# Two edge aggregations: GpSimd's wait for seven of the preceding eight gathers, at every second step only

## The chip, the cores and the metric

The kernel runs on one core of one Trainium2 chip. The metric is the device time of one execution in microseconds (us). Before the change the median of 3 runs is 7060.26 us (7059.98 to 7061.63).

## The reference

The reference is two layers of a graph network on N = 6250 nodes with 256 features each. A layer adds to x a graph attention over E = 200000 edges and a dense mixing of the same rows, and then a mixture of experts. Only the two graph attentions bear on the change. Cut to what matters, layer 0 has

```python
hW = h @ W + b                                   # 6250 x 64
e = leaky_relu(s[row, head] + d[col, head])      # per edge and head, 4 heads
alpha = softmax of e over the edges of one row
out[row, head] += alpha * hW[col]                # sum over the row's edges
```

Layer 1 is the same in form, with a table row of 256 values per node (4 heads x 64) in place of 64. Each edge needs the table row of its column node, and the edges come in no order of columns: this is a gather of 200000 rows, once in each layer.

## The kernel before, in words

The edges are sorted by destination on the chip and padded to 1616 tiles of 128 edges. `stage_aggregate` runs once for each layer (tags `_0` and `_1`, table rows of 68 and of 260 floats). It works in 202 **steps** of KT = 8 tiles, that is 1024 edges, and four steps (STEP_RING = 4, slots r = 0 to 3) make a **turn**. Turn 0 and the last turn (two steps) are written out, the 49 turns between them are a hardware loop.

In every step

- GpSimd (POOL) issues eight indirect DMAs, one for each tile, L876. Each fetches 128 table rows by the indices `st_idx` into `got[:, r, k, :]`, the slot r of a ring of four. The first seven count up the semaphore `gathered[r]`, the eighth `last_in[r]`.
- SyncE loads `spread`, the row numbers of the step's edges, broadcast to all partitions (L893).
- VectorE (DVE) makes the one-hot matrices `hot` (L975) and `hot_t` (L982), and waits for the eight gathers before it reduces the row scores (L993) and makes the exponents `z` (L1002 to L1004, in layer 1 from L995 on).
- ScalarE exponentiates (L909, L912), and DVE scales the gathered rows into `weighted` (L1016), which counts up `scaled`. 
- TensorE (PE) sums the weighted rows by destination with `hot` (L952), DVE adds the sums to `acc` (L1024), and PE makes the scores of a later step (L937).
- Besides, each step takes a part of the layer's dense mixing with it (the "guest": `BallMix` in layer 0, `GateMix` in layer 1), on PE, ACT and DVE. From the middle of the second aggregation the guest is in another phase ("out").

What sets the order on GpSimd is in `gather`, L866 to L877. Before the eight gathers of step j it waits for three things: that ScalarE has staged the step's indices (`idx_staged`), that DVE has scaled step j - 4, so that the slot is free (`scaled`), and that the first seven gathers of step j - 1 have landed (`gathered` of the slot before, L874):

```python
pool.wait_ge(idx_staged, j + 1)
if not first:
    pool.wait_ge(scaled, j - (STEP_RING - 1))
if not first or r > 0:
    t, q = (turn, r - 1) if r else (turn - 1, STEP_RING - 1)
    pool.wait_ge(gathered[q], t * (16 * (KT - 1)) + 16 * (KT - 1))
```

DVE has its own waits for `gathered[r]` and `last_in[r]` ahead of L993.

Of the kernel before, what the change touches and what calls it, by code (L numbers as in the profile page):

```python
# [770 lines left out]
def stage_aggregate(nc, g, tag, table, width, shared, rows, row_list, acc, top, guest):  # L771
# [10 lines left out]
    with stage(nc) as own:  # L782
# [49 lines left out]
        def steps_of(last):  # L832
            return range(ENDING if last else STEP_RING)
# [30 lines left out]
        @block.gpsimd  # L864
        def _(pool):
            def gather(turn, r, first):  # L866
                j = turn * STEP_RING + r
                pool.wait_ge(idx_staged, j + 1)
                if not first:
                    pool.wait_ge(scaled, j - (STEP_RING - 1))  # L870
                if not first or r > 0:
                    t, q = (turn, r - 1) if r else (turn - 1, STEP_RING - 1)
                    pool.wait_ge(gathered[q], t * (16 * (KT - 1)) + 16 * (KT - 1))
                pool.nop(nofuse=True)  # L874
                for k in range(KT):
                    pool.indirect_dma_start(got[:, r, k, :], None, table,  # L876
                                            bass.IndirectOffsetOnAxis(ap=st_idx[:, r, k:k + 1], axis=0))\  # L877
                        .then_inc(gathered[r] if k < KT - 1 else last_in[r], 16)
            for r in range(STEP_RING):
                gather(0, r, True)  # L880
            with pool.Fori(1, TURNS - 1) as turn:
                for r in range(STEP_RING):
                    gather(turn, r, False)
            for r in steps_of(True):
                gather(TURNS - 1, r, False)
# [2287 lines left out]
```

## Time and profile before

| | |
|---|---|
| median of the runs | 7060.26 us |
| profiled execution | 7063.9 us, of which span 7062.1 us |
| first aggregation, first to last gather | 495.4 to 2733 us |
| second aggregation, first to last gather | 3581.8 to 5861.5 us |
| busy share of the span | PE 72%, DVE 62%, POOL 49%, ACT 25% |
| mean granted TensorE clock | 0.83 |

A profile is one execution. Busy is the time in which an engine executes. Idle before an instruction is put down to what ended it: a DMA's landing, another engine's instruction, or "issue", where the profile shows no event that ended it. [...] A wait itself is executed by the engine's sequencer and is idle time of the engine.

### The profile page before, as it was taken

Reading aid. Unit: us, or ns where it says so; the run is one execution under the profiler, and the core shown is the slowest. Engines: PE = TensorE matmul, PEld = TensorE weight load, DVE = VectorE, ACT = ScalarE, POOL = GpSimd, SP = SyncE. Lnnn points to the kernel's source line nnn. Section 1 sums busy time; section 2 is a strip of 40 time slices with the busy share of each in tenths; the row PEclk is TensorE's granted clock in tenths of the full one; section 3 lists DMA queues with packets and bytes.
Section 4 is the critical chain, followed back from the end, with each engine's and each line's share of the span. In section 5 each row is a group of like instructions: output and inputs, shape, how many; then the busy total and the mean of one; then the engine's idle time right before and its main releaser. Section 6 shows DMA issues by size and latency. Waiting matters only on the chain. (4 is left out here: it accounts for less than half of the span.)

```text
span 7062.1 us, 90296 instructions
## 1 busy us (share of the span) xinstructions
PE 5095.9 (72%) x21196; PEld 3660.6 (52%) x21197; DVE 4389.3 (62%) x8953; ACT 1783.8 (25%) x4856; POOL 3469.1 (49%) x3669
## 2 busy tenths in 40 slices
PE   1446666666666664699766666667777777999999
PEld 1445555555555552466534444445555555666666
DVE  8987777777777778722566655556666667333333
ACT  7322222222222222222310000001111113433332
POOL 0126767666767766144146666666666664000000
PEclk8668888888888886799878887877777777999999
DMA  1022222222222222322444444444444444000001
GB/s 55 22 44 51 52 52 52 52 51 52 52 52 52 52 51 58 116 64 64 145 135 124 125 123 123 123 124 130 130 132 132 132 131 114 5 5 4 9 4 36
DMA packets 380644, 534.45 MB, mean 76 GB/s; under 512 B 119264, under 2 KB 240119, under 8 KB 380407
## 3 DMA queue, kind: packets, MB, share of 16 engines
q0 software_dynamic: 139648, 299.92, 17.8%
q1 hardware_dynamic: 240886, 233.29, 11.2%
q8 instruction: 43, 0.70, 0.0%
q14 instruction: 67, 0.54, 0.0%
HBM read 475.96 MB, written 56.96 MB: 75 GB/s over the span
## 5 line engine op out<-in xcount | busy, mean ns | idle before, releaser
L876 POOL DMA_INDIRECT got<-table,st_idx x3232 | 3092.9, 957 | 1453.5 <-issue 1004.8
L952 PE MATMUL ps_sum<-weighted,hot 128*128 128x260 f32 x6464 | 1861.2, 447 | 143.2 <-DVE acc L1024 139.0
L952 PEld LDWEIGHTS ps_sum<-weighted,hot 128*128 128x128 f32 x6464 | 1403.1, 229 | 563.0 <-DVE acc L1024 228.8
L1024 DVE TENSOR_TENSOR acc<-acc,ps_sum 128x260 f32 x1664 | 707.1, 425 | 890.3 <-PE ps_sum L952 750.0
L937 PE MATMUL ps_score<-score_split,hot_t 128*128 x3232 | 250.1, 188 | 1294.7 <-DVE z L1004 1267.5
L937 PEld LDWEIGHTS ps_score<-score_split,hot_t 128*128 128x128 bf16 x3232 | 196.8, 103 | 1471.7 <-issue 1456.7
L1016 DVE TENSOR_TENSOR weighted<-got,ps_weight 128x2048 f32<-128x2048 f32 x404 | 921.5, 2281 | 4.3 <-ACT weighted L912 0.8
L909 ACT ACTIVATE ps_weight<-z 128x32 f32<-128x32 f32 x404 | 81.2, 201 | 2969.8 <-DVE z L1004 2969.8
L3058 DVE SCALAR_TENSOR_TENSOR x_res<-ps_yf,comb,x_res 128x256 f32 x392 | 189.7, 484 | 638.0 <-PE ps_yf L2966 638.0
L975 DVE TENSOR_TENSOR hot<-ps_score,row_loc 128x1024 f32<-128x1024 f32 x404 | 492.1, 1218 | 3.5
L993 DVE TENSOR_REDUCE row_score<-ps_score 128x64 f32<-128x192 f32 (+1 forms) x404 | 163.3, 404 | 520.3 <-DMA got<-table,st_idx 518.9
L2946 PE MATMUL ps_hf<-acc,ws_f 128*128 (+2 forms) x896 | 348.2, 542 | 6.0 <-ACTq L2993 6.0
L2966 PE MATMUL ps_yf<-ws_f,h2t 128*128 128x256 f32 x1568 | 347.7, 379 | 0.8 <-ACT h2t L3006 0.8
L2946 PE MATMUL ps_hf<-h1t,ws_f 128*128 128x384 f32 (+1 forms) x896 | 346.0, 539 | 0.8 <-ACT h1t L3006 0.8
L2966 PEld LDWEIGHTS ps_yf<-ws_f,h2t 128*128 128x128 f32 x1568 | 297.8, 190 | 53.6 <-ACT h2t L3006 1.4
L3006 ACT ACTIVATE h2t<-ps_hf,own_scale 128x512 f32<-128x512 f32 x224 | 162.3, 725 | 507.9 <-PE ps_hf L2946 507.9
L2946 PEld LDWEIGHTS ps_hf<-acc,ws_f 128*128 128x128 f32 x896 | 171.1, 191 | 173.6 <-issue 114.8
L2946 PEld LDWEIGHTS ps_hf<-h1t,ws_f 128*128 128x128 f32 x896 | 170.2, 190 | 156.0 <-issue 107.1
L263 POOL TENSOR_TENSOR shifted<-xs,pivot 128x256 f32<-128x256 f32 x49 | 43.1, 880 | 382.4 <-DVE pivot L401 230.5
L1283 PE MATMUL ps_mix<-mix_xin,wq 128*128 128x128 f32 x1176 | 227.5, 379 | 0.4
L1283 PEld LDWEIGHTS ps_mix<-mix_xin,wq 128*128 128x128 f32 x1176 | 217.7, 289 | 3.7
L1939 POOL DMA_INDIRECT y_rows<-y_e,slot_home x108 | 106.6, 987 | 209.6 <-DVE y_e L2030 205.0
(533 smaller groups left out, 7558.3 us busy)
## 6 DMA issues: line engine op xcount, KB each, us to landing
spread<-row_list SPq DMA_DIRECT2D x404, 256.0 KB
got<-table,st_idx POOLq DMA_INDIRECT x3232, 2.8
gate_xin<-ball_rows SPq DMA_DIRECT2D x98, 128.0 KB
got_y_e<-y_rows SPq DMA_DIRECT2D x10, 896.0 KB
table<-row_e SPq DMA_DIRECT2D x50, 130.0 KB, 2.6
ball_rows<-xt SPq DMA_DIRECT2D x10, 640.0 KB, 4.7
mix_xin<-ball_rows SPq DMA_DIRECT2D x49, 128.0 KB
xn_rows<-xs_m SPq DMA_DIRECT2D x49, 128.0 KB, 1.7
```

Of the source, the lines that this page charges most:

```text
L876: pool.indirect_dma_start(got[:, r, k, :], None, table, bass.IndirectOffsetOnAxis(ap=st_idx[:, r, k:k + 1], axis=0))\
L937: last = nc.tensor.matmul(scores[:, k, :], hot_t[:, r % 2, k, :], split[:, :, :, :].rearrange("p t a c -> p (t a c)")[:, ds(b * SP, SP)], ...
L952: last = nc.tensor.matmul(ps_g[:, p % 2, 0:AW], hot[:, r % 2, k, :], weighted[:, r % 2, k, :], start=(k == n * p), stop=(k == n * p + n - 1))
L975: nc.vector.tensor_tensor(hot[:, r % 2, :, :], count_to.unsqueeze(1).to_broadcast([P, KT, P]), g.row_loc[:, ds(i * KT, KT)].unsqueeze(2).t ...
L993: link(nc.vector.tensor_reduce(row_score[:, :, :], scores.rearrange("p k (a c) -> p k c a", a=PARTS), AX.X, ALU.add))
L1016: nc.vector.tensor_tensor(out, v, w, ALU.mult).then_inc(scaled, 1)
L1024: nc.vector.tensor_tensor(acc[:, ds(b * AW, AW)], acc[:, ds(b * AW, AW)], ps_g[:, p % 2, 0:AW], ALU.add).then_inc(added, 1)
L1283: last = nc.tensor.matmul(bank[:, m * P:(m + 1) * P], self.mix.wq[:, c, (m0 + m) * P:(m0 + m + 1) * P], self.xin[:, c, :], start=(c == 0), ...
L2946: last = nc.tensor.matmul(ps_h[:, j, 0:HALVES[hf][1]], ws[:, par, l, c, f * P:(f + 1) * P], rhs(c, hf), start=(c == 0), stop=(c == 1))
L2966: last = nc.tensor.matmul(ps_y[:, k % 4, 0:D], h2[:, c, k * P:(k + 1) * P], ws[:, par, 2, c, :], start=(c == 0), stop=(c == 1))
L3006: nc.scalar.activation(h[:, f, at:at + n], ps_h[:, j, 0:n], ACT.Relu, bias=own_s[:, par, 1, l, f:f + 1], scale=own_s[:, par, 0, l, f:f + 1])\
L3058: nc.vector.scalar_tensor_tensor(xr, ps_y[:, k % 4, 0:D], comb[:, ds(t * 8 + pair * 2 + par, 1)], xr, ALU.mult, ALU.add).then_inc(y_used, 1)
```

## The change

The wait on `gathered` stands at r = 0 and r = 2 only. At r = 1 and r = 3 the other two waits remain.

```diff
-                if not first or r > 0:
+                if r % 2 == 0 and not (first and r == 0):
                     t, q = (turn, r - 1) if r else (turn - 1, STEP_RING - 1)
                     pool.wait_ge(gathered[q], t * (16 * (KT - 1)) + 16 * (KT - 1))
```

GpSimd's instructions in the loop over the turns, before, from behind the gathers of r = 0 on. A semaphore stands under the first name that its number had in the program: iotas_made is `idx_staged`, x_loaded is `scaled`, and eps0_set, b_wide_ready, w0_prepared and wl_ready are `gathered` of slots 3, 0, 1 and 2, for which the steps r = 0, 1, 2 and 3 wait.

```order
L868 REGISTER_ALU
L870 REGISTER_ALU [waits iotas_made]
L873 ISA [waits x_loaded]
L876 DMA got<-table,st_idx 128x68 [waits b_wide_ready]
L876 DMA got<-table,st_idx 128x68 x7
L868 REGISTER_ALU
L870 REGISTER_ALU [waits iotas_made]
L876 DMA got<-table,st_idx 128x68 [waits x_loaded,w0_prepared]
L876 DMA got<-table,st_idx 128x68 x7
L868 REGISTER_ALU
L876 DMA got<-table,st_idx 128x68 [waits wl_ready,iotas_made,x_loaded]
L876 DMA got<-table,st_idx 128x68 x7
```

And the same piece with the change:

```order
L868 REGISTER_ALU
L870 REGISTER_ALU [waits iotas_made]
L876 DMA got<-table,st_idx 128x68 [waits x_loaded]
L876 DMA got<-table,st_idx 128x68 x7
L868 REGISTER_ALU
L870 REGISTER_ALU [waits iotas_made]
L873 ISA [waits x_loaded]
L876 DMA got<-table,st_idx 128x68 [waits w0_prepared]
L876 DMA got<-table,st_idx 128x68 x7
L868 REGISTER_ALU
L876 DMA got<-table,st_idx 128x68 [waits iotas_made,x_loaded]
L876 DMA got<-table,st_idx 128x68 x7
```

The first gather of r = 1 no longer waits for slot 0's gathers, and that of r = 3 no longer for slot 2's. No gather moves; the empty instruction L873 only goes to another step. The same holds for the second aggregation, whose rows read 128x260.

The first turn, which is written out ahead of the loop, as the difference of the two:

```order
 L876 DMA got_0<-table0,st_idx_0 128x68 [waits iotas_made]
 L876 DMA got_0<-table0,st_idx_0 128x68 x7
-L876 DMA got_0<-table0,st_idx_0 128x68 [waits iotas_made,b_wide_ready]
+L876 DMA got_0<-table0,st_idx_0 128x68 [waits iotas_made]
 L876 DMA got_0<-table0,st_idx_0 128x68 x7
 L876 DMA got_0<-table0,st_idx_0 128x68 [waits iotas_made,w0_prepared]
 L876 DMA got_0<-table0,st_idx_0 128x68 x7
-L876 DMA got_0<-table0,st_idx_0 128x68 [waits iotas_made,wl_ready]
+L876 DMA got_0<-table0,st_idx_0 128x68 [waits iotas_made]
 L876 DMA got_0<-table0,st_idx_0 128x68 x7
```

Here too only the waits of the second and the fourth step are gone. Of the 201 such waits of an aggregation 101 go and 100 stay. The other engines' instructions are the same.

## Rows read from the trace of the kernel before

**Rows 1.** Costliest groups: busy us, mean ns of one | idle before it, its enders.

```profile
L876 POOL DMA_INDIRECT got<-table,st_idx x3232 | 3092.9, 957 | 1453.5 <-issue 1004.8 <-DMA got<-table,st_idx 398.6 <-ACT st_idx L904 32.1
```

**Rows 2.** Busy by stretch: us, PE PEld DVE ACT POOL (count), PEclk, DMA share, GB/s.

```profile
497.00:2734.00 2237.00, 1496.74 (x7455) 1221.13 (x7456) 1641.97 (x2810) 594.20 (x2021) 1558.14 (x1615) 0.83 0.25 52
3583.00:4710.00 1127.00, 751.72 (x2866) 486.48 (x2866) 680.67 (x1296) 77.74 (x395) 758.15 (x799) 0.80 0.45 124
4710.00:5862.00 1152.00, 856.51 (x3169) 621.62 (x3169) 723.61 (x1434) 216.74 (x548) 773.98 (x817) 0.75 0.47 130
```

**Rows 3.** POOL's timeline, start us, us, [idle before]: one turn, second aggregation, r = 0 first.

```profile
4304.57 0.94 POOL L876 DMA_INDIRECT got<-table,st_idx  x1 [1.34 <-DMA got<-table,st_idx]
...
4313.32 0.94 POOL L876 DMA_INDIRECT got<-table,st_idx  x1 [0.30 <-issue]
4315.75 0.95 POOL L876 DMA_INDIRECT got<-table,st_idx  x1 [1.48 <-DMA got<-table,st_idx]
...
4324.50 0.95 POOL L876 DMA_INDIRECT got<-table,st_idx  x1 [0.30 <-issue]
4326.76 0.94 POOL L876 DMA_INDIRECT got<-table,st_idx  x1 [1.31 <-issue]
...
4335.51 0.94 POOL L876 DMA_INDIRECT got<-table,st_idx  x1 [0.30 <-issue]
4337.84 0.94 POOL L876 DMA_INDIRECT got<-table,st_idx  x1 [1.39 <-DMA got<-table,st_idx]
```

**Rows 4.** Groups of L876 without the first gather: first aggregation, then the second.

```profile
L876 POOL DMA_INDIRECT got<-table,st_idx x1615 | 1558.1, 965 | 678.4 <-issue 494.8 <-DMA got<-table,st_idx 165.5 <-DVE weighted L1016 17.4
L876 POOL DMA_INDIRECT got<-table,st_idx x1615 | 1532.1, 949 | 746.4 <-issue 510.0 <-DMA got<-table,st_idx 233.1 <-ACT st_idx L904 2.7
```

**Rows 5.** POOL's timeline: four of the 36 long gaps at a step's second gather.

```profile
653.26 0.95 POOL L876 DMA_INDIRECT got<-table,st_idx  x1 [1.68 <-issue]
...
1503.87 0.94 POOL L876 DMA_INDIRECT got<-table,st_idx  x1 [1.68 <-issue]
...
1626.01 0.94 POOL L876 DMA_INDIRECT got<-table,st_idx  x1 [1.68 <-issue]
...
5853.10 0.94 POOL L876 DMA_INDIRECT got<-table,st_idx  x1 [1.67 <-issue]
```

**Rows 6.** Groups of L993: first aggregation, then the second to 4710, then from 4710.

```profile
L993 DVE TENSOR_REDUCE row_score<-ps_score 128x64 f32<-128x192 f32 x201 | 71.4, 355 | 297.4 <-DMA got<-table,st_idx 296.9
L993 DVE TENSOR_REDUCE row_score<-ps_score 128x96 f32<-128x288 f32 x99 | 45.0, 455 | 147.1 <-DMA got<-table,st_idx 147.0
L993 DVE TENSOR_REDUCE row_score<-ps_score 128x96 f32<-128x288 f32 x102 | 46.1, 452 | 75.8 <-DMA got<-table,st_idx 75.0
```

**Rows 7.** Timeline of DVE and PE around one wait for gathers, second aggregation.

```profile
5218.12 0.48 DVE L982 TENSOR_SCALAR hot_t<-spread,lane 128x1024 bf16<-128x1024 bf16 x1
...
5221.32 0.46 DVE L993 TENSOR_REDUCE row_score<-ps_score 128x96 f32<-128x288 f32 x1 [2.72 <-DMA got<-table,st_idx]
...
5223.03 0.62 PE L937 MATMUL ps_score<-score_split,hot_t 128*128 x8 [4.75 <-DVE z L1004]
```

**Rows 8.** Who waited for whom: us in total, times, longest us; whole span.

```profile
POOL got L876 <- ACT st_idx L904: 32.1, 13, 16.4
...
POOL got L876 <- DVE weighted L1016: 18.0, 16, 1.6
```

**Rows 9.** L876 over the span: duration ns min/median/max; then time to landing.

```profile
L876 POOL DMA_INDIRECT got<-table,st_idx x3232: 938/944/1446, 495.4 to 5860.6; - x191
...
DMA to landing us min/median/max: 2.3/2.8/4.7
```

**Rows 10.** Timeline, first aggregation: a gather beside hot_t; the group of hot_t.

```profile
1522.86 0.48 DVE L982 TENSOR_SCALAR hot_t<-spread,lane 128x1024 bf16<-128x1024 bf16 x1
1522.98 1.17 POOL L876 DMA_INDIRECT got<-table,st_idx  x1 [0.30 <-issue]
...
L982 DVE TENSOR_SCALAR hot_t<-spread,lane 128x1024 bf16<-128x1024 bf16 x202 | 101.6, 503 | 0.1
```

## The prediction

> **What bounds the kernel now.** I read the busy shares by stretch first, then the groups of gathers, then GpSimd's timeline of single steps, and last what the consumers wait for. In the two aggregations no engine is full: by stretch PE is busy 67 to 74% of the time, DVE 60 to 73%, GpSimd 67 to 70%, and the DMA engines 25 to 47% [rows 2]. A busy share does not tell the bound here, since GpSimd's gathers come one after another with fixed gaps. The 3232 gathers are busy for 3092.9 us and have 1453.5 us of idle time before them, which together is the length of both aggregations [rows 1]. So the step is as long as eight gathers and the gaps before them.
>
> The timeline shows what the gaps are [rows 3]. Within a step each gather follows the last one after 0.30 us, which no event ended: about 0.94 + 0.305 = 1.25 us per gather, 10.0 us per eight. Ahead of the first gather of a step the gap is 1.31 to 1.48 us, and what ends it is the landing of gathers. That is the wait on `gathered`: the seventh gather of the step before lands some time after the eighth has been issued, and the sequencer then starts the next one. The turn repeats in all 50 turns of an aggregation. (The row at 4326.76 says "issue", but its wait is the same one; so "issue" holds a part of these pauses.)
>
> That the gathers set the end is seen on the other side: DVE waits for them ahead of L993 for 296.9 us in the first aggregation and for 147.0 + 75.0 us in the second [rows 6]. During such a wait PE does nothing either: its next matmul, the score, comes after 4.75 us of idle time and is released by the same DVE's `z` [rows 7]. A shorter wait is thus a shorter step, not one that PE fills.
>
> **The change part by part.** Removed are 101 pauses in each aggregation, at r = 1 and r = 3. Nothing is added: no gather, no DMA and no instruction of another engine, and on GpSimd's queue nothing is moved past anything. With the wait gone, the first gather of such a step should follow like the others, after 0.305 us, since the two waits that remain were nearly always over long before: `scaled` ended a gap 16 times in 404 steps, 18.0 us in all, and `idx_staged` 13 times, 32.1 us, of which 16.4 us is a single wait at the stage's start [rows 8].
>
> First aggregation: idle time before 1615 gathers is 678.4 us [rows 4]. Less 1615 x 0.305 = 492.6 us of plain gaps, 185.8 us are left. A second kind of gap has to come off: 18 times the second gather of a step comes after 1.68 us in place of 0.30 [rows 5], 18 x 1.37 = 24.7 us. So 161.1 us belong to 201 pauses, 0.80 us each over the plain gap. Half of them go: **81 us**.
>
> Second aggregation: 746.4 - 492.6 - 24.7 = 229.1 us, 1.14 us each; half is **115 us**. In the turn shown the odd pauses are the longer ones, 1.48 + 1.39 against 1.34 + 1.31 us [rows 3], less 0.305 each 2.26 against 2.04 us, 5% over the mean of both: **+5 us**.
>
> The kept pauses, at r = 0 and r = 2, I cost at no change: they end by the landing of the seventh gather of the step before, median 2.8 us after issue [rows 9], and gathers already follow each other at 1.25 us in each run of eight. So two or three are under way at any time, then as now, though 16 come in a run. The DMA engines are busy 45 to 47% in the second aggregation [rows 2]; some 5% more in the same time does not fill them.
>
> What is late next is DVE, with PE behind it. Its wait for gathers is the cover that the gain can use up: 296.9 us for 81 in the first aggregation, 147.0 for about 59 in the first half of the second, but 75.0 for about 61 in the second half, where the guest is heavier [rows 6]. DVE is not late in every step there, and the ring of four slots evens out only neighbours; carrying the 102 steps forward with DVE's own time per step as it is and the gathers earlier, I find that 8 us are not given back: **-8 us**.
>
> Sum: 81 + 115 + 5 - 8 = 193 us. Against the profiled execution's 7063.9 us this is 6871 us; the median stands 3.6 us below that execution, so I predict **6867 us** (-2.7%). Bounds of the sum: at best nothing is lost to DVE and the clock, granted at 0.75 in the last stretch [rows 2], comes up with the shorter idle times to the 0.80 of the stretch before. That shortens PE's 856.5 us there by 54 us; I let a third of it count, since DVE waits for PE only in part, and the gain is 193 + 8 + 19 = 220 us, about 6840 us. At worst that stretch gives back nothing, 193 - 53 = 140 us (61 less the 8 already off), 6920 us.
>
> One thing in the trace speaks against the change. A gather is longer where DVE's `hot_t` starts just before it: 1.17 us beside the 0.94 us of the others, and up to 1.446 us, a lengthening of 0.50 us, as long as a `hot_t` takes [rows 9, 10]. Now some `hot_t` fall into a pause of GpSimd, where they cost nothing. The means of 965 and 949 ns against the median of 944 [rows 4, 9] put today's cost at 34 and 8 us. With a random place of `hot_t` in the step I expect about the same, and enter 0; the worst is that each of the 202 steps without a pause meets a full one, 202 x 0.50 = 101 us, which the rivals take up. [...]
>
> **The rivals.**
>
> *DVE and PE take it back* (8%). In the second half of the second aggregation PE is busy 74%, and DVE's waits on gathers are down to 75.0 us in 102 steps [rows 2, 6]. If its time per step grows where the wait shrinks, that half gains nothing: 6920 us. Against it stands that PE idles during the waits [rows 7].
>
> *The lock costs what the pause saved* (3%): 193 - 101 = 92 us gained, 6968 us. For it: the rows on `hot_t`. Against it: most gathers beside a `hot_t` show no lengthening (the mean in the second aggregation is 949 ns).
>
> *The wait only changes its name* (3%): `scaled` or `idx_staged` would be reached at once, and the time is 7060 us within 14. Against it are the few times that either ended a gap [rows 8].
>
> *Slower: long runs of gathers cost a stall* (6%). Once in 88 gathers, 18 times in each aggregation, the gap at L876 is 1.68 us though nothing is waited for [rows 5]; from 1503.87 to 1626.01 are 88 gathers. Something is counted there. If it is descriptors that pile up while GpSimd does not pause, and the pauses now clear it, a run of 16 would meet such a stall each time: 202 x 1.37 = 277 us against 193 gained, 7144 us. It decides for slower from a stall in 70% of the runs (193 / 277). Against it: 88 gathers hold eleven of today's pauses, the interval is the same in both aggregations though their transfers differ almost fourfold in size, and within a run of eight the eighth gather takes no longer than the first, 0.94 us [rows 3].
>
> **How the numbers follow.** The forecast has 80%, the rivals 8, 3, 3 and 6%. The range is 6840 to 6945 us: the bounds of the sum, 6840 and 6920, with 25 us above for a part of the lock's price. It holds the first rival and nearly all of the forecast's chance; left out are the other rivals and some 5% of the forecast. A measurement of this kernel can tell about 0.2%, 14 us, from no change. Faster by more than that: 80 + 8 + 3 = 91%; within it 3%; slower 6%.
>
> **What would show it.** Right: in the first gathers of r = 1 and r = 3 the gap is 0.30 us, in those of r = 0 and 2 it stays at 1.0 to 1.4; L876 idles some 80 us less in the first aggregation and 115 to 120 less in the second; the aggregations take about 2157 and 2168 us; DVE's wait at L993 falls to about 215 and 110 us, and all other stages stay as they are. Wrong: gathers longer than 965 ns in the mean (lock); more than 36 gaps of 1.68 us (stall); gaps at r = 1 and 3 that end by `weighted` or `st_idx` (another name); GpSimd idle less but the second aggregation no shorter (DVE and PE). Kept pauses that grow by as much as the others shrink would refute the costing of landings.

## The result, and the profile after

The changed kernel takes 6814.94 us (median of 4 runs, 6807.93 to 6820.05), the kernel before 7060.53 us in the same comparison: a ratio of 0.9651, 95% interval 0.9635 to 0.9668. It is 246 us faster, where 193 us were forecast, and the time lies 25 us below the range. The profiled execution is the lowest of the four, 6807.93 us with a span of 6806.1 us, so the two traces differ by 256 us.

Busy time by stretch of the changed kernel, as in [rows 2]: us, busy of PE, PEld, DVE, ACT and POOL with counts, granted TensorE clock, share of the DMA engines, GB/s. The first row is the first aggregation, the other two are the halves of the second.

```profile
494.50:2613.00 2118.50, 1463.42 (x7445) 1189.48 (x7445) 1637.79 (x2812) 593.29 (x2021) 1544.21 (x1616) 0.85 0.25 55
3466.00:4533.00 1067.00, 727.22 (x2898) 483.46 (x2898) 688.22 (x1308) 78.10 (x398) 766.35 (x808) 0.82 0.48 133
4533.00:5602.00 1069.00, 829.13 (x3125) 599.61 (x3125) 711.76 (x1412) 215.49 (x543) 765.45 (x808) 0.77 0.50 138
```

From first to last gather the aggregations now take 2118.7 and 2136.9 us, before 2238.0 and 2279.8: 119 and 143 us less, and all the rest of the kernel 6 us more. The granted clock is up by 0.02 in each stretch: 0.85, 0.82 and 0.77, before 0.83, 0.80 and 0.75 [rows 2].

GpSimd's timeline over one turn of the second aggregation, r = 0 first, as in [rows 3]:

```profile
4142.25 0.94 POOL L876 DMA_INDIRECT got<-table,st_idx  x1 [1.25 <-DMA got<-table,st_idx]
...
4151.00 0.95 POOL L876 DMA_INDIRECT got<-table,st_idx  x1 [0.30 <-issue]
4152.26 0.95 POOL L876 DMA_INDIRECT got<-table,st_idx  x1 [0.30 <-issue]
...
4163.31 0.95 POOL L876 DMA_INDIRECT got<-table,st_idx  x1 [1.25 <-DMA got<-table,st_idx]
...
4173.30 0.95 POOL L876 DMA_INDIRECT got<-table,st_idx  x1 [0.30 <-issue]
...
4184.34 0.94 POOL L876 DMA_INDIRECT got<-table,st_idx  x1 [1.34 <-DMA got<-table,st_idx]
```

The steps r = 1 (4152.26) and r = 3 (4173.30) begin 0.30 us after the last gather, like any other gather; r = 0 and r = 2 still pause. The gathers' groups of the two aggregations, to be held against [rows 4]:

```profile
L876 POOL DMA_INDIRECT got<-table,st_idx x1615 | 1543.4, 956 | 573.8 <-issue 472.5 <-DMA got<-table,st_idx 98.9 <-DVE weighted L1016 1.8
L876 POOL DMA_INDIRECT got<-table,st_idx x1615 | 1531.8, 948 | 603.9 <-issue 470.6 <-DMA got<-table,st_idx 127.5 <-DVE weighted L1016 4.9
```

And DVE's wait for gathers, in the groups over the whole span, against [rows 6]:

```profile
L993 DVE TENSOR_REDUCE row_score<-ps_score 128x64 f32<-128x192 f32 (+1 forms) x404 | 162.7, 403 | 340.7 <-DMA got<-table,st_idx 339.8
```

The idle time fell by 104.6 and 142.5 us, more than the 81 and 120 us that the removed pauses were to bring. And in the first aggregation the gathers themselves are shorter, 956 ns for 965, 14.7 us in all. DVE still waits for gathers, 339.8 us for 519.

Where the rest of the idle time went is seen at the long gaps of [rows 5]. The first gathers of the steps 14, 25 and 36, with the second gather of each:

```profile
640.46 0.94 POOL L876 DMA_INDIRECT got<-table,st_idx  x1 [1.00 <-DMA got<-table,st_idx]
643.08 1.19 POOL L876 DMA_INDIRECT got<-table,st_idx  x1 [1.68 <-issue]
...
756.40 0.94 POOL L876 DMA_INDIRECT got<-table,st_idx  x1 [0.30 <-issue]
757.65 0.94 POOL L876 DMA_INDIRECT got<-table,st_idx  x1 [0.30 <-issue]
...
871.11 0.94 POOL L876 DMA_INDIRECT got<-table,st_idx  x1 [0.96 <-DMA got<-table,st_idx]
873.72 0.94 POOL L876 DMA_INDIRECT got<-table,st_idx  x1 [1.68 <-issue]
```

Before, each of these steps had a gap of 1.68 us ahead of its second gather. Now step 25, which begins without a wait, has none. Nine are left in each aggregation, all in steps that begin with a wait, where 18 were before.

The third source is the pause that was kept. The mean gap ahead of a step's first gather, taken over all steps of the trace, in us:

| | first aggregation, r = 0 and 2 | r = 1 and 3 | second, r = 0 and 2 | r = 1 and 3 |
|---|---|---|---|---|
| before | 1.118 | 1.101 | 1.384 | 1.514 |
| changed | 0.998 | 0.305 | 1.301 | 0.305 |

The kept pauses are 0.12 and 0.08 us shorter, 100 of each. So three things had to be explained: long gaps, kept pauses and shorter gathers.

### The profile page after: what moved, and what is told of

Read it like the earlier page. It is cut to its first block and busy times, and to the rows that moved or that the text cites. A ratio compares the mean times of both kernels' runs of the same rounds, so it can differ in the third digit from the quotient of the medians.

```text
span 6806.1 us, 90196 instructions
## 1 busy us (share of the span) xinstructions
PE 5017.1 (74%) x21196; PEld 3608.0 (53%) x21197; DVE 4385.5 (64%) x8953; ACT 1781.6 (26%) x4856; POOL 3454.1 (51%) x3669
## 5 line engine op out<-in xcount | busy, mean ns | idle before, releaser
L876 POOL DMA_INDIRECT got<-table,st_idx x3232 | 3077.8, 952 | 1205.1 <-issue 943.1
L1016 DVE TENSOR_TENSOR weighted<-got,ps_weight 128x2048 f32<-128x2048 f32 x404 | 921.5, 2281 | 4.3 <-ACT weighted L912 0.8
L993 DVE TENSOR_REDUCE row_score<-ps_score 128x64 f32<-128x192 f32 (+1 forms) x404 | 162.7, 403 | 340.7 <-DMA got<-table,st_idx 339.8
## 6 DMA issues: line engine op xcount, KB each, us to landing
spread<-row_list SPq DMA_DIRECT2D x404, 256.0 KB
```

Of the source, the lines that this page charges most:

```text
L876: pool.indirect_dma_start(got[:, r, k, :], None, table, bass.IndirectOffsetOnAxis(ap=st_idx[:, r, k:k + 1], axis=0))\
L993: link(nc.vector.tensor_reduce(row_score[:, :, :], scores.rearrange("p k (a c) -> p k c a", a=PARTS), AX.X, ALU.add))
L1016: nc.vector.tensor_tensor(out, v, w, ALU.mult).then_inc(scaled, 1)
```

## The experiments

**The wait at the odd steps** in place of the even ones.

```diff
-                if not first or r > 0:
+                if r % 2 == 1:
```

> The wait stands at r = 1 and r = 3 only, the other half of the steps; nothing is left out. After the change 9 long gaps of 1.68 us at a step's second gather were left in each aggregation, at the steps 14, 36, 58 and so on, where 18 stood before, at 14, 25, 36 and so on. Theory A (every eleventh step the sequencer is held up for about 1.4 us whatever the step; it shows only where the sequencer has just come out of a wait and has nothing issued ahead): 9 long gaps in each aggregation, but now at the odd steps 25, 47, 69. Theory B (the hold-up belongs to the number of pauses, one for each eleven of them): 9 gaps at even steps again, or at steps of another interval. The kept pauses now are those at r = 1 and 3, which met the spread loads before: theory C (a kept pause is longer where a spread load is under way) expects them at 1.1 us in the first and 1.4 to 1.5 us in the second aggregation, against 1.00 and 1.30 in the changed kernel, and a time of 6820 to 6850 us; if the spread loads don't matter, 1.00 and 1.30 us and the time of the changed kernel, 6815 us.

6849.3 us, ratio 0.9706 (0.9689 to 0.9722). Steps 14 and 25 again, in this kernel's timeline of GpSimd:

```profile
640.73 0.94 POOL L876 DMA_INDIRECT got<-table,st_idx  x1 [0.31 <-issue]
641.98 0.96 POOL L876 DMA_INDIRECT got<-table,st_idx  x1 [0.30 <-issue]
...
756.27 0.95 POOL L876 DMA_INDIRECT got<-table,st_idx  x1 [1.04 <-DMA got<-table,st_idx]
758.89 0.94 POOL L876 DMA_INDIRECT got<-table,st_idx  x1 [1.67 <-issue]
```

Theory A holds: the gap went from step 14 to step 25, and on to 47, 69 and so on, nine in each aggregation. The hold-up is there every eleventh step, and it shows only behind a wait. Why is seen in the sequencer's own rows. When its branch at the end of a turn is executed, gathers that it has issued have not yet begun on the engine: four or five in the kernel before and here, eight to ten in the changed kernel. So a delay of 1.37 us (1.68 - 0.305) is covered by gathers already issued. Directly behind a wait nothing is: in the trace before, each of the 402 waits ends after the last gather issued ahead of it (at one of them 4303.86 against 4303.22 us, and the next gather begins at 4304.57). The covered hold-up shows there too: in the first aggregation of the changed kernel it is eight gathers in the turns 11, 22, 33 and 44, whose last steps 47, 91, 135 and 179 are such eleventh steps without a wait, and ten in all the other 45 turns of the loop.

The kept pauses are 1.058 us in the first aggregation (1.1 was expected) and 1.533 in the second (1.4 to 1.5). In the first, those of r = 3 now end by `scaled` for the most part, 46.7 us. Of the first aggregation's pauses those of r = 1, which end by a landing, stand at 1.002, so 1.1 us was not met there. With nearly the same number of waits (101 in place of 100) this kernel is 34 us slower than the change: which half of the waits is kept matters. The largest part is idle time ahead of the second aggregation's gathers, 628.8 us against 603.9; gathers that are 12 and 4 us longer in sum, 1555.2 and 1536.0 us, add to it.

**No wait at all** on the preceding gathers.

```diff
-                if not first or r > 0:
-                    t, q = (turn, r - 1) if r else (turn - 1, STEP_RING - 1)
-                    pool.wait_ge(gathered[q], t * (16 * (KT - 1)) + 16 * (KT - 1))
```

> The wait on the preceding step's gathers stands nowhere; only the waits for the indices and for the free slot are left. Nothing is left out. Theory (each pause costs its gap less 0.305 us, and the long gaps are hidden wherever there is no pause): no gap over 0.31 us at a step's first gather save for late indices or slots, no gap of 1.68 us, gathers at 1.25 us each. From the changed kernel's 6815 us the first aggregation gains 70 us of pauses and 12 of long gaps; the second has 100 us of pauses and 12 of long gaps, but DVE waits only 110.6 us for gathers in its first half and 30.0 in its second, so I expect 55 and 25 there: 6650 us, range 6620 to 6700, with GpSimd now waiting for DVE's scaled in the last stretch. Rival (with no pause at all gathers pile up at the DMA engines): landings of 4 us or more in the median against 2.7, gathers longer than 952 ns in the mean, and a time of 6815 us or more.

6634.01 us, ratio 0.9401 (0.9386 to 0.9417), inside the range: 424 us faster than the kernel before, at 7057.51 us in that comparison, and some 180 us faster than the change, so the best version here. The groups of its gathers, first and second aggregation (the line is 873 here):

```profile
L873 POOL DMA_INDIRECT got<-table,st_idx x1615 | 1543.4, 956 | 492.5 <-issue 492.5
L873 POOL DMA_INDIRECT got<-table,st_idx x1615 | 1536.7, 952 | 492.4 <-issue 491.5 <-DVE weighted L1013 0.9
```

The view of that line's instructions over the span, with their duration (min/median/max in ns) and the time to landing:

```profile
L873 POOL DMA_INDIRECT got<-table,st_idx x3232: 943/947/1445, 494.5 to 5411.0; - x191
...
DMA to landing us min/median/max: 2.3/2.8/5.2
```

All idle time left in each aggregation is 1615 gaps of 0.305 us. No long gap is left, the sequencer is twelve gathers ahead at the end of every turn, gathers land after 2.8 us in the median as before, and their means of 956 and 952 ns are those of the changed kernel within 4 ns. The rival of piled-up gathers falls. My expectation that DVE would hold GpSimd back in the last stretch fell too: `scaled` ended a wait for 0.9 us in all. DVE is later at the very end instead: its last add to `acc` ends 38.4 us after the last gather of the second aggregation, where it was 24.5 us in the kernel before.

**Small spread loads**, all waits kept.

```diff
-                sp.dma_start(spread[:, r % SPREAD_RING, :], row_list[ds(i, 1), :].to_broadcast([P, KT * P])).then_inc(spread_in[r % SPREAD_RING], 16)
+                n, q = P if first and r < SPREAD_RING else 16, r % SPREAD_RING
+                sp.dma_start(spread[0:n, q, :], row_list[q:q + 1, :].to_broadcast([n, KT * P])).then_inc(spread_in[q], 16)
```

> The kernel before, all waits kept, but from the third step on the load of spread fills 16 partitions in place of 128, always with the row numbers of step 0 or 1: row scores of all later steps are those of wrong rows, so this part of the computation is left out. SyncE issues the same number of loads at the same places. Theory C (a pause is longer where a spread load delays the seventh gather's landing): the long pauses go, the mean pause falls from 1.109 us to about 1.00 in the first and from 1.449 to about 1.30 us in the second aggregation, both at even and at odd steps; 22 + 30 = about 50 us less in all, near 7010 us. If the spread loads don't matter the pauses stay at 1.11 and 1.45 us and the time at 7060 us.

7044.46 us in a single run, 13 us under the median of the kernel before in that comparison (7057.51). The gathers' groups:

```profile
L876 POOL DMA_INDIRECT got<-table,st_idx x1615 | 1567.5, 971 | 659.8 <-issue 490.2 <-DMA got<-table,st_idx 168.0 <-DVE weighted L1017 1.0
L876 POOL DMA_INDIRECT got<-table,st_idx x1615 | 1532.8, 949 | 735.9 <-issue 506.2 <-DMA got<-table,st_idx 227.6 <-ACT st_idx L905 2.1
```

The mean pauses are 0.993 (even steps) and 1.038 us (odd) in the first aggregation, 1.307 and 1.484 in the second. At the even steps that is what the changed kernel shows, 0.998 and 1.301, so the spread loads did make these pauses longer. But 50 us were expected, and two things take them away: the gathers of the first aggregation came out longer, 971 for 965 ns, which gives 9 of its 19 us back, and the odd pauses of the second hardly moved: 1.484 us is also what other kernels with all waits there show (1.479 in run e4, 1.481 in run e6). Another cause had to be there.

**Small loads of the guest too.** In the kernel before, SyncE's load of `gate_xin` is issued beside the seventh gather of an even step, at 4312.07, and the pause behind it is 1.48 us [rows 3]:

```profile
4311.88 0.33 SPq L2467 DMA_DIRECT2D gate_xin<-ball_rows  x1
4312.07 0.95 POOL L876 DMA_INDIRECT got<-table,st_idx  x1 [0.30 <-issue]
```

```diff
-            sp.dma_start(self.xin[:, h, :, :], mix.f_t[ds(j, 1), :, :, :].rearrange("o p c n -> (o p) c n")).then_inc(self.x_in, 16)
+            n = 16
+            sp.dma_start(self.xin[0:n, h, :, :], mix.f_t[ds(j, 1), 0:n, :, :].rearrange("o p c n -> (o p) c n")).then_inc(self.x_in, 16)
```

(and the same for tile i, from the third on)

> As the run with the small spread loads (all waits kept, row numbers left out from the third step on), and besides the guest's loads of gate_xin in the second aggregation fill 16 partitions in place of 128 from the third tile on, so that the dense mixing of layer 1 is left out in part too. With small spread loads alone the pauses of the second aggregation stayed at 1.46 and 1.51 us at r = 1 and 3, against 1.31 and 1.30 at r = 0 and 2, and gate_xin is issued at every second step, about when the seventh gather is. Theory C, widened to all of SyncE's loads: 1.30 us at r = 1 and 3 too, about 18 us less in the second aggregation, 7025 us. If gate_xin is not the cause: 1.46 and 1.51 us as there, and 7044 us.

7030.01 us in a single run. The same turn in its timeline, r = 1, 2, 3 and 0:

```profile
4295.96 0.95 POOL L876 DMA_INDIRECT got<-table,st_idx  x1 [1.30 <-DMA got<-table,st_idx]
...
4306.97 0.94 POOL L876 DMA_INDIRECT got<-table,st_idx  x1 [1.32 <-issue]
...
4318.10 0.94 POOL L876 DMA_INDIRECT got<-table,st_idx  x1 [1.45 <-DMA got<-table,st_idx]
...
4329.15 0.95 POOL L876 DMA_INDIRECT got<-table,st_idx  x1 [1.29 <-DMA got<-table,st_idx]
```

r = 1 is down from 1.46 to 1.33 us in the mean and on the level of r = 0 and 2 (1.31); r = 3 fell from 1.51 to 1.43 and keeps 0.12 us over them. So a load of SyncE beside the seventh gather goes with a later landing, and the pause shows it. For `spread`: in the trace before the seventh gather lands 2.735 us after its start where a load is issued within the 1.75 us behind that start, and 2.507 us after it elsewhere (even pauses of the first aggregation; 3.038 and 2.790 in the second), with the small loads of run e3 2.496 and 2.437 (2.824 and 2.762). For `gate_xin`, at the odd pauses of the second aggregation: 3.103 and 2.875 us in run e1, whose loads are whole, 2.820 and 2.782 here. The rest at r = 3 is open; it is there in the first aggregation too (1.10 against 1.00 at r = 1), whose guest loads were left as they are.

**More instructions on GpSimd**, to see what the long gap counts.

```diff
+                for _ in range(4):
+                    pool.sem_inc(spare, 1)
                 pool.wait_ge(idx_staged, j + 1)
```

> The kernel before, all waits kept, with four increments of a spare semaphore more on GpSimd ahead of each step's waits. Nothing is left out. It asks what the long gap of 1.68 us counts, which comes every eleventh step, 88 gathers apart. If gathers (or their descriptors) are counted: 18 long gaps in each aggregation, still 88 gathers apart. If instructions of GpSimd's sequencer are counted: more of them, closer together, 88 x 46 / 62 = about 65 gathers apart and some 24 in each aggregation, at places that are no longer always the second gather. The time is 7060 us plus at most 12 us either way; each increment itself takes some tens of ns of the sequencer, which runs ahead of the engine.

7059.03 us in a single run. The trace has the increments: each takes 17 ns on GpSimd's sequencer, the four begin 78 ns apart, and at most steps the first is executed when five gathers of the step before have not yet begun on the engine (GpSimd's rows at L870 and L879). The long gaps stay 18 in each aggregation, 88 gathers apart, at the second gather of the same steps; step 25 here (the line is 879):

```profile
773.13 0.95 POOL L879 DMA_INDIRECT got<-table,st_idx  x1 [1.67 <-issue]
```

Not the number of instructions sets the interval but that of gathers, or something each of them brings. The first long gap stands ahead of the 114th gather in both aggregations, so a count of gathers does not run on from one aggregation to the next (1832 indirect DMAs lie between, no multiple of 88). What is done in these 1.4 us stays open.

**Another form of hot_t**, all waits kept.

```diff
-                nc.vector.tensor_scalar(..., spread[:, r % SPREAD_RING, :], g.lane[:, 0:1], None, ALU.is_equal)
+                nc.vector.tensor_tensor(..., spread[:, r % SPREAD_RING, :], g.lane[:, 0:1].to_broadcast([P, KT * P]), ALU.is_equal)
```

> The kernel before, all waits kept, with hot_t made by a tensor_tensor of spread and a broadcast of lane in place of the tensor_scalar with a scalar operand; nothing is left out. DVE needs about 1.2 us for it in place of 0.503 (the tensor_tensor that makes hot takes 1.218). Theory D (the tensor_scalar on bf16, and not any DVE work, lengthens a gather that begins beside it): the mean gather falls from 965 to 950 ns in the first aggregation (a rest stays beside L1016 and L1423) and from 949 to 946 in the second, and the time by the 24 + 5 us that this makes of 2 x 1616 gathers, less what a longer DVE step gives back: 7030 to 7055 us. Rival (any DVE operation at that place lengthens it, or it is the place in the step): the means stay at 965 and 949 and the time at 7060 or some us above, for 0.7 us more of DVE per step.

7145.13 us, ratio 1.0126 (1.0109 to 1.0143), slower, and neither theory had that. The groups of gathers and of hot_t over the span:

```profile
L876 POOL DMA_INDIRECT got<-table,st_idx x3232 | 3216.5, 995 | 1408.9 <-issue 1009.1 <-DMA got<-table,st_idx 348.0 <-ACT st_idx L904 32.8
L982 DVE TENSOR_TENSOR hot_t<-spread,lane 128x1024 bf16<-128x1024 bf16 x404 | 491.4, 1217 | 5.9 <-DMA spread<-row_list 5.6
```

One pair of them in its timeline:

```profile
3705.76 1.22 DVE L982 TENSOR_TENSOR hot_t<-spread,lane 128x1024 bf16<-128x1024 bf16 x1
3705.83 1.95 POOL L876 DMA_INDIRECT got<-table,st_idx  x1 [1.31 <-DMA got<-table,st_idx]
```

The gather that begins 0.07 us after hot_t lasts 1.95 us in place of 0.94, so it is about 1 us longer, beside a hot_t that still had 1.15 us to run. Theory D, that only the tensor_scalar does this, falls: the tensor_tensor does it too, and for longer. The busy time of all gathers is up by 123.6 us (3216.5 - 3092.9), shorter gaps give 44.6 us back (1453.5 - 1408.9), which together is 79 us; the traced span is up by 79.9 us (7062.1 to 7142.0), the median by 89 us. So here the lengthened gathers went straight into the time, which is what the 14.7 us of shorter gathers in the changed kernel need. Four of the long gaps came out shorter here, 0.63 to 0.99 us: each stands behind a lengthened gather of 1.63 to 1.98 us and is shorter by as much as that gather is longer. So in these four the hold-up ran on while the engine worked, as theory A has it.

**The change in the first aggregation only.**

```diff
-                if not first or r > 0:
+                if r % 2 == 0 and not (first and r == 0) if shared else not first or r > 0:
```

> The change in the first aggregation only, at r = 1 and r = 3; the second keeps its wait at every step. Nothing is left out. Theory (each aggregation's gain is the sum of its own gaps, and nothing else of the kernel moves): the first aggregation's gathers span 2119 us as in the changed kernel, the second's 2280 us as in the kernel before, and the time is 7060 - 119 + 4 = 6945 us (6938 to 6952). Rival (a part of the gain in the second aggregation came from the first one's change, or the reverse): more than 8 us off.

6942.35 us, ratio 0.9837 (0.9821 to 0.9854).

```profile
L876 POOL DMA_INDIRECT got<-table,st_idx x1615 | 1544.1, 956 | 575.0 <-issue 472.4 <-DMA got<-table,st_idx 100.2 <-DVE weighted L1016 1.5
L876 POOL DMA_INDIRECT got<-table,st_idx x1615 | 1532.7, 949 | 744.4 <-issue 511.1 <-DMA got<-table,st_idx 229.4 <-ACT st_idx L904 2.4
```

The first row is that of the changed kernel within 1.2 us, shorter gathers included, the second that of the kernel before within 2. The two aggregations gain independently, 114 us for the first by this measurement.

## Why the prediction was right in kind and too small

| term | predicted, us | measured, us | how |
|---|---|---|---|
| removed pauses, first aggregation | 81 | 80 | 101 x (1.101 - 0.305) |
| removed pauses, second | 115 + 5 | 122 | 101 x (1.514 - 0.305) |
| kept pauses | 0 | 20 | 100 x 0.120 + 100 x 0.083 |
| long gaps | 0 | 25 | 18 x 1.37 |
| length of the gathers | 0 | 15 | 14.7 + 0.3 |
| given back by DVE | -8 | -8.5 | last add after last gather: 19.3 to 23.6 us, 24.5 to 28.7 us |
| sum | 193 | 254 | the spans differ by 256.0 |

The mechanism was right: the step is as long as its gathers and gaps, and a removed pause is a shorter step. The two terms that carried the sum came out within 2 us. The loss to DVE also had its size, but by luck: it was forecast where DVE would hold GpSimd up in the last stretch, and GpSimd was hardly held up; in its place each aggregation ends some 4 us later after its last gather.

What failed in the prediction are three terms set to zero, and all of them were gains.

- "A second kind of gap has to come off", 18 x 1.37 us in each aggregation. I took these off the pauses, rightly, and then let them stand after the change. But they showed only directly behind a wait, where nothing is issued ahead; at the ends of the turns four to twelve gathers were. Runs e1 and e2 show it: the gaps follow the wait from even to odd steps, and without a wait there are none. Half of them went, 25 us. The rival "slower", in which long runs would meet such a stall each time, had it the wrong way round.
- "The kept pauses, at r = 0 and r = 2, I cost at no change". They end by a landing, and the landing came 0.23 and 0.25 us later beside a `spread` load (small loads bring the even pauses to the same 0.99 and 1.31 us). With half of the waits gone those loads lie beside other gathers, whose landing nobody waits for. The two traces show the shift: before, SyncE issues a `spread` load within 1.75 us behind the start of the seventh gather ahead of 40 and 24 of the 100 even pauses of the two aggregations, and these last 1.254 and 1.540 us in the mean, the others 1.026 and 1.335; in the changed kernel it does so ahead of 4 and 2. Small loads lie there as often (52 and 29 in run e3) and make no more than 0.04 us of it. That is 14 of the 20 us (40 x 0.228 + 24 x 0.205); the rest stays open.
- "With a random place of hot_t in the step I expect about the same, and enter 0". The gathers became 15 us shorter, and hot_t was only the smaller part of it. What the gathers of the first aggregation lasted beyond 945 ns (those over 985 ns counted) is 34.2 us before, and only 7.9 us of it lie in gathers beside hot_t, which runs when they begin or starts within 0.06 us. 23.4 us lie beside three tensor_tensors of the guest, L1409, L1417 and L1423. In the changed kernel it is 19.9 us, 2.8 and 15.2 of them. So the guest's operations fell beside the beginning of a gather less often (8.2 us), and hot_t too (5.1 us). The longest gather, from which the 0.50 us of the bound were taken, stands beside L1423 in the trace before; beside hot_t no gather there is lengthened by more than 0.25 us:

```profile
2030.63 0.69 DVE L1423 TENSOR_TENSOR mix_o<-mix_den,mix_qs 128x512 f32<-128x512 f32 x1
2030.69 1.45 POOL L876 DMA_INDIRECT got<-table,st_idx  x1 [0.30 <-issue]
2031.24 2.28 DVE L1016 TENSOR_TENSOR weighted<-got,ps_weight 128x2048 f32<-128x2048 f32 x1
2032.44 0.94 POOL L876 DMA_INDIRECT got<-table,st_idx  x1 [0.30 <-issue]
```

What the prediction calls the lock is the lengthening of a gather beside `hot_t`. No run of the change shows its price of 101 us, or the 25 us that the range has for a part of it: in the two aggregations 7.9 + 4.3 us lie beside hot_t before, and 2.8 + 3.5 us in the changed kernel.

The argument that most gathers beside a hot_t show no lengthening was a misreading: of 53 gathers of the first aggregation that begin with 0.2 us or more of hot_t left, 47 last over 985 ns. That the term came out as a gain is luck, though it comes again with the same change (14.0 us in run e6): run e1, with its waits at the other half of the steps, got 2.9 us back in the first aggregation and lost 3.9 in the second.

The bounds failed with them. The best case gave 19 us for a clock of 0.80, which was my estimate (a third of 54 is 18), and nothing for these three, which make 60 us together, so the range began 25 us too high. The clock rose from 0.75 to 0.77 in the last stretch (0.78 in run e2, without any wait), and since GpSimd was not held up there, nothing of the gain can be put down to it.

The rivals: DVE and PE did not take the gain back, and not even without any wait; the waits did not change their names (`scaled` ended gaps for 1.8 + 4.9 us); gathers are longer beside hot_t, by up to 1.04 us in run e5 and 0.25 us before, but that was met less often, not more.

## What to carry to other kernels

Here the wait of an issuing engine cost more than its own gap: directly behind it nothing was issued ahead, and delays of 1.37 us came out that were covered elsewhere, 18 in each aggregation before and nine with half of the waits. When such a wait is taken away, look for every gap that occurs only just behind it, and bound a term that "does not change" from both sides like any other. Then try the change to its end: half of the waits gave 246 us, all of them 424.

## What was not expected of the hardware

Every 88 gathers, ahead of the 114th of an aggregation first, the gap at a step's second gather is 1.68 us in place of 0.305 where the step begins with a wait, whatever the size of the gathers (68 or 260 floats a row) and unchanged by four more instructions of GpSimd's sequencer a step (18 in each aggregation before and in run e4, nine in the changed kernel and in run e1, none in run e2).

Gathers that begin just after a DVE tensor_tensor of 128x1024 bf16 last up to 1985 ns against a median of 945 (run e5), 1.04 us longer; beside the tensor_scalar that does the same work it is up to 0.25 us (1192 ns, before). The guest's f32 tensor_tensors, both of whose inputs lie in SBUF, go with longer gathers as well (1.45 us above). Of the 636 gathers in the trace before that begin with 0.2 us or more of L1016 left, which is longer (2.28 us) but has its second input in PSUM, none lasts over 957 ns. What makes the difference no run here takes apart.
